# One block for all engine programs of a four-layer attention and mixture-of-experts kernel

## The reference

```
# layer 0: self attention, cross attention, mixture of experts (8 experts, 2 per row)
q = ln(x);  x = x + mha(q, q);  x = x + mha(ln(x), ln(ctx))
h = ln(x);  vals, idx = top_k(h @ rw.T + rb, 2);  gates = softmax(vals)
x = x + sum_k gates[k] * expert[idx[k]](h)          # expert: fc2(gelu(fc1(h)))
# layer 1: only the 10 rows of each batch with the highest score attend to ctx
idx = top_k(x @ score_w, 10);  x[idx] = mha(x[idx], ctx)
# layer 2: rms norm, rotary embedding, grouped attention with mask, gated silu
x = x + softmax(rope(q) @ rope(k).T / 8 + mask) @ v @ Wo
x = x + (silu(rms(x) @ Wgate) * (rms(x) @ Wup)) @ Wdown
# layer 3: cross attention with weights rounded to three levels
x = x + mha(ln(x), ctx, Wo = bit_quant(Wo), ...)
```

## Time and profile before

| what | value |
|---|---|
| timed runs | 1375.11, 1377.88 (median), 1378.68 us |
| profiled execution | 1374.12 us |
| its span | 1372.3 us |
| granted TensorE clock, mean | 0.934 of full |
| PE / PEld busy | 1223.7 us (89%) / 1033.4 us (75%) |
| DVE / ACT / POOL busy | 728.3 (53%) / 611.6 (45%) / 429.3 us (31%) |

### The profile page before, as it was taken

One profiled execution on the slowest core, in us unless ns is written; L12 is line 12 of the kernel. 1 busy time (PEld: TensorE's weight loads), 2 busy tenths in 40 slices (PEclk: granted clock), 3 DMA queues, 4 the chain that ended last, 5 costly groups with the idle time before them and its releaser, 6 DMA issues. The chain is left out here.

```text
span 1372.3 us, 36268 instructions
## 1 busy us (share of the span) xinstructions
PE 1223.7 (89%) x14778; PEld 1033.4 (75%) x14778; DVE 728.3 (53%) x1677; ACT 611.6 (45%) x1464; POOL 429.3 (31%) x545
## 2 busy tenths in 40 slices
PE   4899999876899999999678869999999999988986
PEld 2566666655689989999567759889889898866665
DVE  3688887767322000000565367567567567526775
ACT  2455565421545445445212235445445445425552
POOL 3224446343222222235200034424434333232200
PEclk9999999965899999999866789999999999999997
DMA  9000000000589999998510010100101101000000
GB/s 310 2 2 2 2 2 17 17 9 24 153 292 331 336 347 355 355 347 292 178 33 2 2 40 25 36 21 25 36 21 31 30 22 30 12 1 1 17 21 28
DMA packets 91573, 130.74 MB, mean 95 GB/s; under 512 B 13392, under 2 KB 74064, under 8 KB 91280
## 3 DMA queue, kind: packets, MB, share of 16 engines
q1 hardware_dynamic: 85360, 117.11, 26.1%
q0 software_dynamic: 4768, 10.26, 2.1%
q10 hardware_dynamic: 1280, 1.04, 0.2%
HBM read 116.82 MB, written 11.57 MB: 94 GB/s over the span
## 5 line engine op out<-in xcount | busy, mean ns | idle before, releaser
L1794 ACT ACTIVATE w_ca<-scores,fc1b 128x128 f32<-128x128 f32 x312 | 114.4, 368 | 140.9 <-PE scores L1749 120.1
L1749 PEld LDWEIGHTS scores<-reg 128*128 128x128 f32 x1248 | 146.8, 194 | 7.4 <-DMA reg<-in_fc 3.1
L1749 PE MATMUL scores<-reg 128*128 128x128 f32 x1248 | 147.6, 277 | 4.4 <-DMA reg<-in_fc 2.3
L858 DVE TENSOR_REDUCE reg<-scores 128x8 f32<-128x1024 f32 x96 | 113.1, 1220 | 65.0 <-PE scores L499 64.5
L2369 ACT ACTIVATE reg<-reg,mx 128x128 f32<-128x128 f32 x256 | 99.3, 389 | 105.4 <-DVE mx L2520 105.4
L1828 DVE TENSOR_TENSOR reg<-bank,reg 128x256 f32<-128x256 f32 x39 | 16.6, 425 | 242.0 <-PE bank L1759 233.7
L1759 PE MATMUL bank<-reg,w_ca 128*128 128x256 f32 x624 | 141.1, 379 | 0.3 <-DVE small L1819 0.3
L1759 PEld LDWEIGHTS bank<-reg,w_ca 128*128 128x128 f32 x624 | 115.6, 190 | 14.5 <-DVE small L1819 0.3
L1442 PEld LDWEIGHTS scores<-reg 128*128 128x128 f32 x1024 | 116.7, 192 | 2.1 <-ACT reg L2377 1.4
L1442 PE MATMUL scores<-reg 128*128 128x128 f32 x1024 | 117.1, 275 | 0.5 <-ACT reg L2377 0.5
L2299 PE MATMUL bank<-reg,w_ca 128*128 128x256 f32 x496 | 115.3, 385 | 0.1
(11 more groups left out here) (304 smaller groups left out, 2384.6 us busy)
## 6 DMA issues: line engine op xcount, KB each, us to landing
reg<-in_fc SPq DMA_DIRECT2D x78, 1024.0 KB, 7.8
w_sa<-grouped_values SPq DMA_DIRECT2D x64, 128.0 KB, 2.6
reg<-expert_out SPq DMA_DIRECT2D x16, 256.0 KB, 4.1
xres<-in_x SPq DMA_DIRECT2D x4, 512.0 KB, 10.9
ctxr<-in_ctx SPq DMA_DIRECT2D x1, 2048.0 KB, 14.8
w_l<-in_w_l SPq DMA_DIRECT2D x2, 1024.0 KB, 12.2
routed_rows<-reg SPq DMA_DIRECT2D x8, 256.0 KB, 2.1
grouped_values<-reg SPq DMA_DIRECT2D x16, 128.0 KB, 1.7
```

What stands on the lines that cost most here:

```text
L858: ins = nc.vector.tensor_reduce(mxpad.rearrange("p (c n d) -> p n c d", c=C, d=DH)[:, 4 * half:4 * half + 4, :, 0], scores4[:, 2 * half:2 ...
L1749: ins = nc.tensor.matmul(S[n % 4][:, 0:P], up_w8[j % 2][:, c, f * P:(f + 1) * P], xbT[:, j % 2, c, :], start=(c == 0), stop=(c == C - 1))
L1794: nc.scalar.activation(h1[:, j % 2, f, :], S[n % 4][:, 0:P], ACT.Gelu, bias=fc1b[:, bass.ds(e * FC + f, 1)]).then_inc(M["fc1_free"], 1)
```

## The change

There is one block for all programs, opened ahead of the first attention. It closes when the function ends. The three `with nc.Block` lines go, and with them borders 1, 2 and 3. The wait for the stores moves to the end of SyncE's program of layer 3. No other line changes, but for its indentation, and every semaphore wait stays. Lines move by one or two: what is `L499` before is `L500` after, `L1738` is `L1739`. The diff without indentation:

```diff
@@ -350,4 +350,6 @@
                                      den_inv[:, :, :].unsqueeze(3).to_broadcast([P, 8, 2, DH])))
 
+        block = ctx.enter_context(nc.Block(no_gpsimd_drain=True))
+
         def attention(stages, store=False, router=None, begun=None):
@@ -463,5 +465,4 @@
             first_program = not cross(0)
 
-            with nc.Block(no_gpsimd_drain=True) as block:
                 @block.tensor
                 def _(pe):
@@ -966,4 +967,5 @@
                             sp.dma_start(out.rearrange("b p d -> p b d")[:, 2 * p:2 * p + 2, :],
                                          xres[:, 2 * p:2 * p + 2, :]).then_inc(stored, 16)
+                    sp.wait_ge(stored, 16 * (B // 2))
@@ -2604,8 +2605,4 @@
         attention([dict(q_norm=("l3_g", "l3_b"), kv="raw", w=w_l3, bq="l3_bq", bk="l3_bk", bv="l3_bv", ob="l3_ob",
                         loads=["l3", "ctx"])], store=True, begun=last)
-        with nc.Block(no_gpsimd_drain=True) as block:
-            @block.sync
-            def _(sp):
-                sp.wait_ge(stored, 16 * (B // 2))
```

More of the change, by code:

```diff
@@ L953, in _ @@
[L953 to L967 removed]
+                            project("q1", g, P, hT_a)
@@ new lines, in _ @@
+            @block.sync
+            def _(sp):
+                if first_program:
+                    first_rows(sp)
+                    load_the_rest(sp)
+                    for q in range(B // 2):
+                        store_routed(sp, q)
+                if router is not None:
+                    router.first_loads(sp)
+                if store:
+                    sp.wait_ge(M["l3_open"], 1)
+                    for p in range(B // 2):
+                        await_moved(sp, ("y", p))
+                        sp.dma_start(out.rearrange("b p d -> p b d")[:, 2 * p:2 * p + 2, :],
+                                     xres[:, 2 * p:2 * p + 2, :]).then_inc(stored, 16)
+                    sp.wait_ge(stored, 16 * (B // 2))
@@ new lines, in _ @@
+        @block.sync
+        def _(sp):
+            load_down(sp, 0)
+            load_down(sp, 1)
+            for j in range(NBLK):
+                if j + 2 < NBLK:
+                    sp.wait_ge(M["turned_in"], j + 1)
+                    if j + 4 < NBLK:
+                        load_ids(sp, j + 4)
+                    sp.wait_ge(M["fc1_full"], FC * (j + 1))
+                    load_up(sp, j + 2)
+                if j >= 1 and j + 1 < NBLK:
+                    sp.wait_ge(M["fc2_full"], j)
+                    load_down(sp, j + 1)
+                if j == 0:
+                    sp.wait_ge(ld["xn"], 16 * B // 2)
+                if j in grouped_at:
+                    load_grouped(sp, grouped_at[j])
@@ new lines, in scores_turned @@
+            def scores_turned(g):
+                pe.wait_ge(M["tok_sub_ok"], g + 1)
+                for s in range(2):
+                    for c in range(C):
+                        for j in range(GB):
+                            for r in range(4):
+                                a0 = (2 * s + c) * P + j * R
+                                ins = nc.tensor.matmul(S[r][:, a0:a0 + R], tok_K[g % 3][tok_rows(r), s, c, keys_of(j)],
+                                                       tok_Q[tok_rows(r), g % 2, s, c, mine(j)], start=True, stop=True)
+                ins.then_inc(M["tok_st_full"], 1)
@@ new lines, in _ @@
+            bank = tok_claim(pe, ("bias", 0))
+            pe.wait_ge(M["y_ok"], NBLK - 1)
+            pe.wait_ge(M["tok_bv_ok"], C)
+            for c in range(C):
+                ins = nc.tensor.matmul(bank[:, 0:D], tok_bv[:, c * P:(c + 1) * P], w_l1[:, c, 3 * D:4 * D],
+                                       start=(c == 0), stop=(c == C - 1))
+            ins.then_inc(tok_done(("bias", 0)), 1)
+            turn_ctx(0, 2)
+            turn_ctx(1, 2)
+            keys(0, 2)
+            keys(1, 2)
```

2523 lines of the change are left out of this document (1234 added, 1289 removed).

## The result

| kernel | median us | lowest to highest | runs | ratio to before | profiled execution | span |
|---|---|---|---|---|---|---|
| before | 1372.95 | 1368.14 to 1381.43 | 20 | | 1374.12 | 1372.3 |
| after (one block) | 1368.58 | 1363.15 to 1375.60 | 20 | 0.9950 [0.9934, 0.9966] | 1366.74 | 1365.0 |

Single executions of one kernel differ by up to 13 us, so the size of the change depends on how it is computed: the ratio in the table, over all runs, is -6.9 us (-9.1 to -4.7) of 1373, the medians differ by 4.4 us, the means (1374.2 and 1368.1) by 6.1 us, and the two profiled executions by 7.4 us. I go by the ratio and its interval. The forecast change was -6.4 us. The forecast time, 1371.5 us, is 2.9 us too long: the three runs it started from had a median of 1377.88, and the 20 runs of the same kernel, those three among them, have 1372.95.

What follows compares the result with a forecast made beforehand. PE (TensorE, busy 89%) bounds the kernel; the second border holds up GpSimd, and GpSimd holds up PE. Terms -0.4 - 6.0 + 0 = -6.4 us, from a three-run median of 1377.88 to 1371.5 us; range 1366.1 to 1376.5.

Steps and rivals of the forecast that it cites:

- Border 2, the gaps and the clock: Layer 2 to last attention: PE's idle 1.48 and 4.04 us go (-5.5), and PE stays at 2.4 GHz (-0.9).
- GpSimd has slack of 11 us: Last attention: GpSimd's normalisations done at about 1215.4, 11 us before PE's transposes of group 1 ask for them.
- The held operation: VectorE's last normalised rows of layer 2 take about 0.8 us instead of 0.354, held by GpSimd's bias addition: +0.4 us.
- Border 1: First attention to experts: PE starts at 366.10 instead of 366.47 and the experts' stage keeps it, -0.4 us.
- Border 3 and the jumps: Border just before the end, under the last store's flight, and each engine's jump to its next program: 0 us.
- layer 1's clock: Rivals, 660 to 850 us: one group at the high level -2.8 us (chance 0.11), at 1.2 GHz +2.8 (worse clock 0.13).
- GpSimd still late: Rival at the last attention's transposes: PE still waits about 4 us, 1376.4 us; chance 0.10 together with no effect.
- PE stopping at the jump: Same rival's other form: PE stops at the jump to its next program, so only the second gap closes; shares that 0.10.
- no effect: Rival: some wait of the next program stands where the border stood, 1377.9 us; shares the 0.10 of GpSimd still late.

Runs made afterwards that it cites:

- before_again: The kernel before, unchanged, profiled a second time; from layer 2's last values to the first scores 5.17 us, from there to the turned scores 15.65 us.
- after_again: The one-block kernel, unchanged, run again for a second profile; 1362.40 us, ratio to before 0.9947 [0.9920, 0.9974].
- mid_first: One-block kernel with GpSimd's last-attention program first waiting until VectorE has scaled layer 2's last rows; 1363.68 us, ratio to before 0.9954 [0.9931, 0.9978].
- b1_kept: One-block kernel with only the border between the first attention and the experts put back; 1364.83 us, ratio to before 0.9950 [0.9928, 0.9971].
- b2_pool_ahead: Border between layer 2 and last attention kept, GpSimd's first part of that attention moved ahead of it; 1362.47 us, ratio to before 0.9940 [0.9919, 0.9961].
- b3_kept: One-block kernel with only the border behind the last attention put back; 1361.30 us (9 runs), ratio to before 0.9934 [0.9909, 0.9958].

## Why the prediction went as it did

- *Border 2, the gaps and the clock (-5.5 - 0.9): right.* E + F went from 20.83 to 14.20, -6.63; before_again against after_again gives the same. The transposes start 5.74 us earlier behind the last values (5.5 forecast: I had added starts and durations, and rows that follow each other without a stop overlap by 0.07 to 0.16 us in the trace). Behind the transposes 0.89 us are gained, with the clock at 1.00 (0.9 forecast). What I saw as two gaps with two causes was one: GpSimd's start decides, and PE's 1.48 us lay within.
- *GpSimd has slack of 11 us: right* (1214.60 against 1225.31; mid_first delays it and nobody waits). VectorE's work beside the moved operations wasn't slowed beyond the one that I named: its statistics take 0.39 to 0.43 us and its 128x512 additions 0.69 in both profiles.
- *The held operation (+0.4): right mechanism, too large.* Its length is as forecast (0.8 us), its cost 0.13 us.
- *Border 1 (-0.4): right, 0.46 at its place and 0.31 to 0.43 at the second expert step.* ScalarE's end to PE's start was 0.05 us and not 0.14. I took the gain as kept through the experts; that isn't shown. PE waits for weights in that stage (0.5 to 3.5 us), and b1_kept has the same ratio as the one-block kernel, within 0.2%.
- *Border 3 and the jumps (0): right.* 2.6 and 2.7 us at the end; no idle time of PE at the jump to the last attention in any profile without border 2. The Trainium skill (Advanced Engine Details and Errata, § ISA Cache) gives lines of 256 instructions, two of them, and also 128 KB on TensorE against 32 KB elsewhere; the prediction left the second figure out. That a jump's target may be missing was my conclusion from the first. These jumps of PE show no stop.
- *Sum.* -0.46 - 6.63 + 0.13 = -6.96 by the rows, -6.9 [-9.1, -4.7] by the ratio, -6.4 forecast. No large miss hides another: nearly all of the difference is the held operation (0.27) and the idle stretches (0.24), and both go the same way.
- *The step that failed is the last one:* "The median of the three timed runs is 1377.88, 3.8 us over the profiled one; I keep the difference". Three runs of a program that varies by 13 us gave a median 4.9 us above that of 20, and I treated it as an offset of the profiler. Chance is enough for that: of all triples from the 20 runs, 27% have a median of 1377.88 or more. The profiled execution, 1374.12, lies inside the spread and 1.2 us above the 20-run median, not 3.8 below the kernel's time. On the profiled execution alone the sum gives 1367.7 us and on the 20-run median 1366.6, against 1368.58 measured. The spread was in the profile before: I had priced layer 1's clock at 2.8 us a group as a rival and didn't apply it to the base. Nor does the base hold from chip to chip: the one-block kernel has 1368.58 us in one set and 1362.40 in another, with the same ratio.
- *The rivals.* GpSimd still late, PE stopping at the jump, and no effect: excluded by E and F. Layers 1 and 2 do vary by more than the change (D: 552.6 to 559.9), but 4.6 and 5.0 us of it lie between two executions of one kernel; no run shows that the change steers it.

Open: what sets the clock's level where it varies, what else A and C vary by, and whether the gain at border 1 reaches the end.

## What to carry over

- A barrier costs what the latest engine could have done before it. Find the engine that has been idle longest behind its last instruction and whose first work behind the barrier others wait for; PE's own idle time at the barrier may be the smaller part, and lie inside the other.
- The barrier needn't always go: moving that engine's work ahead of it recovered 5.10 of 6.63 us here.
- Put a sum on a ratio or on many runs. A median of three runs says nothing finer than the spread of the program; locate that spread (in which stretch, at which clock) before adding an offset.

## What the runs showed of the hardware

- The granted clock fell behind a stop of PE of 4.04 and of 5.22 us (0.57 over 2 us, 0.73 over 8 us), and not behind one of 1.48 us (1.00, b2_pool_ahead). It also fell behind one of 1.72 us in b3_kept (0.61 over 4 us), where the kernel after kept 1.00 behind 1.73.
- A 128x256 scaling by VectorE took 0.354 us alone, 0.81 beside a GpSimd addition of 0.7 us and 1.12 beside a GpSimd multiplication of 1.04 us; on the path only 0.13 us of the 0.46 counted.
- PE stood 1.48 us at border 2 and 1.15 at border 1, the same to 0.01 us in every profile that has them (four and three). Without the border it was 0 and 0.69.
- Time went with the mean granted clock: a correlation of -0.85 over 35 runs of one kernel on one chip.
